# Spreading a head pair's projections one by one over the attention stage, and two output buffers for three in the expert projection (8 cores)

## What is computed

```python
xn = layernorm(x)
Q, K, V = xn @ Wq, xn @ Wk, xn @ Wv            # 16 heads of 64
alpha = softmax(Q @ K.T / 8)                   # over all keys
alpha = where(causal, alpha, 0)                # masked after the softmax
s = alpha @ V
# expert attention: 8 experts, width 128, router mask m and weights rw
q, k, v = [einsum('tc,ecd,te->td', xn, w, m) for w in (q_proj, k_proj, v_proj)]
ao = causal_softmax(q @ k.T / sqrt(128)) @ v
g = silu(einsum('td,edc,te->tc', ao, o_proj, m * rw))
out = x + s * g
```

## Time and profile before

| | |
|---|---|
| median of 2 runs | 3564.84 us (3513.45 and 3616.22) |
| the profiled execution | 3513.46 us, span 3511.6 us on its slowest core (core 6) |
| spans of the 8 cores | 3494.2 to 3511.6 us |
| TensorE matmuls | 2532.0 us busy, 72% |
| TensorE weight loads | 1156.4 us, 33% |
| VectorE | 2273.3 us, 65% |
| ScalarE | 2114.9 us, 60% |
| GpSimd | 256.7 us, 7% |

### The profile page before, as it was taken

How to read it: one execution, slowest core, us unless ns; L and a number is a source line. 1 busy time by engine, 2 the same in 40 slices (tenths; PEclk the granted TensorE clock), 3 DMA queues, 4 the chain that set the end, 5 groups by cost and what they waited for, 6 DMA issues and landing times.

```text
span 3511.6 us, 59735 instructions; the slowest of 8 cores (3494.2 to 3511.6 us)
## 1 busy us (share of the span) xinstructions
PE 2532.0 (72%) x18500; PEld 1156.4 (33%) x18642; DVE 2273.3 (65%) x5890; ACT 2114.9 (60%) x2466; POOL 256.7 (7%) x706
## 2 busy tenths in 40 slices
PE   2179997675677777777777777777777877886651
PEld 1134444332233333333333333333333333332220
DVE  7447774233366776776677677667766766776764
ACT  0000003521177986897798689779868977996762
POOL 0100000000000000010000001000000100011012
PEclk9999998898878778867877876887787578655555
DMA  5510000113200000000000000000000000003346
GB/s 154 142 40 1 1 1 1 55 52 112 83 3 3 6 6 3 4 9 3 3 6 6 3 4 9 3 3 6 6 3 4 9 3 3 6 6 113 109 147 208
DMA packets 35776, 117.11 MB, mean 33 GB/s; under 512 B 5778, under 2 KB 5778, under 8 KB 35474
## 3 DMA queue, kind: packets, MB, share of 16 engines
q1 hardware_dynamic: 22738, 71.34, 6.0%
q0 software_dynamic: 12736, 41.95, 4.1%
HBM read 79.72 MB, written 33.55 MB: 32 GB/s over the span
## 4 chain that ended last, share of the span: by engine, by line
PE 31%; ACT 21%; issue 14%; DVE 11%; another core or an unknown queue 10%; DMA 7%; DVEq 4%; POOL 0%; ACTq 0%; SPq 0%; POOLq 0%
ACT expC L1342 7%; ACT stagef L1357 6%; PE PB L887 5%; PE PB L901 5%; PE PB L872 5%; PE PB L804 4%; PE PB L759 3%; PE PB L801 3%; PE PB L816 3%; ACT stagef L1342 3%; ACT R L1357 3%; DVE tmpc L1205 2%; DMA KTt<-s_sp 2%; DVEq L1273 2%
## 5 line engine op out<-in xcount | busy, mean ns | idle before, releaser
L1205 DVE TENSOR_REDUCE tmpc<-stagef 128x2 f32<-128x1024 bf16 (+2 forms) x726 | 811.4, 1127 | 235.9 <-ACT stagef L1357 179.4
L1342 ACT ACTIVATE expC<-PB 128x1024 bf16<-128x1024 f32 x768 | 853.3, 1111 | 87.3 <-PE PB L887 87.3
L1357 ACT ACTIVATE stagef<-PB 128x1024 bf16<-128x1024 f32 x600 | 667.8, 1113 | 204.8 <-PE PB L901 132.2
L1205 DVE TENSOR_REDUCE tmpc<-R 128x2 f32<-128x1024 bf16 (+2 forms) x362 | 406.2, 1122 | 118.2 <-ACT R L1357 89.9
L1342 ACT ACTIVATE stagef<-PB 128x1024 bf16<-128x1024 f32 x384 | 429.2, 1118 | 73.4 <-PE PB L887 73.4
L887 PE MATMUL PB<-R 64*128 64x512 bf16 x1152 | 299.9, 508 | 228.2 <-ACT stagef L1357 134.5
L887 PE MATMUL PB<-QTt,KTt 64*128 64x512 bf16 x1152 | 285.8, 484 | 146.0 <-ACT stagef L1357 78.6
L1357 ACT ACTIVATE R<-PB 128x1024 bf16<-128x1024 f32 x296 | 329.9, 1114 | 81.8 <-PE PB L901 60.6
L681 PE MATMUL PB<-R,xnT 128*128 128x512 bf16 x1504 | 336.5, 380 | 2.8 <-DVE lnat L998 1.1
L1322 ACT ACTIVATE expC<-PB 128x512 bf16<-128x512 f32 x144 | 74.6, 610 | 364.3 <-remote 343.7
L901 PE MATMUL PB<-R 64*128 64x512 bf16 (+3 forms) x1088 | 265.0, 479 | 36.4 <-ACT expC L1342 19.2
(11 more groups left out here) (162 smaller groups left out, 2948.2 us busy)
## 6 DMA issues: line engine op xcount, KB each, us to landing
stagef<-x SPq DMA_DIRECT2D x64, 512.0 KB, 4.3
out<-Vau SPq DMA_DIRECT2D x32, 512.0 KB, 3.0
g_sp<-stagef SPq DMA_DIRECT2D x32, 256.0 KB, 2.0
s_sp<-s_stage POOLq DMA_DIRECT2D x64, 128.0 KB, 2.4
QTt<-g_sp POOLq DMA_DIRECT2D x32, 256.0 KB, 5.5
KTt<-s_sp POOLq DMA_DIRECT2D x32, 256.0 KB, 5.6
R<-qp POOLq DMA_DIRECT2D x8, 512.0 KB, 5.5
R<-kp POOLq DMA_DIRECT2D x8, 512.0 KB, 4.6
```

The source lines that it names most:

```text
L1205: e.tensor_reduce(s.tmpc[:].rearrange("p (h c) -> p h c", h=2)[:, :, c:c + 1], s.c1scr((m1 - 1) % 3)[:, 0:2 * kw] .rearrange("p (h k) -> p ...
L1342: e.activation(s.expCs(es), PB[[0, 1, 3][it["slot"]]][:, :], AF.Exp).then_inc(sem["aC2"], 1)
L1357: e.activation(scr[:, 0:1024], pbsrc[:, 0:1024], AF.Exp).then_inc(sem["aC1"], 1)
```

## The change

It has two parts. In `build_p3_items` a QKV item now follows every 15th C1 or C2 item, never two in one place, and not within two C2 items behind the one that ends a query block (`cool`). A place that this rule forbids is skipped. Whatever is left goes ahead of the last item of the pair. In the expert output projection the buffers are `PB[0]` and `PB[1]` in turn, not three, and the wait for the Silu is one tile tighter. Nothing else changes: the same items, the same instructions in each.

```diff
--- before.py
+++ after.py
@@ -181,14 +181,22 @@
             qk = qkv_items(p + 1)
             merged = []
             qi = 0
+            cool = 0
             for idx2, it in enumerate(base):
+                if idx2 == len(base) - 1:
+                    while qi < len(qk):
+                        merged.append(qk[qi])
+                        qi += 1
                 merged.append(it)
-                if qi < len(qk) and idx2 >= 30 and (idx2 - 30) % 14 == 0:
+                if it["kind"] == "C2":
+                    if it["t"] == 4 * it["j"] + 3:
+                        cool = 2
+                    elif cool > 0:
+                        cool -= 1
+                if (qi < len(qk) and idx2 >= 30 and (idx2 - 30) % 15 == 0
+                        and cool == 0):
                     merged.append(qk[qi])
                     qi += 1
-                    if qi < len(qk) and (idx2 - 30) % 28 == 0:
-                        merged.append(qk[qi])
-                        qi += 1
             while qi < len(qk):
                 merged.append(qk[qi])
                 qi += 1
@@ -750,9 +758,9 @@
                                    s.idt_bf[:])
             last.then_inc(sem["tT4"], 1)
             e.wait_ge(sem["aE4"], qt + 1)
-            if qt >= 3:
-                e.wait_ge(sem["aS4"], qt - 2)
-            pbo = PB[qt % 3]
+            if qt >= 2:
+                e.wait_ge(sem["aS4"], qt - 1)
+            pbo = PB[0] if qt % 2 == 0 else PB[1]
             last = None
             for ei in range(8):
                 for half in range(2):
```

## The result

The changed kernel takes 3535.08 us in the median of 43 runs (3530.65 to 3656.24), the kernel before 3516.08 us in 42 (3506.43 to 3628.03). The ratio is 1.0061, 95% interval 1.0054 to 1.0068: 21 us more. Some executions of every kernel take a few per cent longer at a lower granted clock on one die (the trace of transposes_later is of such a one): the medians hold them, and the ratios compare the others. The prediction was 3507 us, 7 us less than before: the size is small as forecast, the sign is wrong.

What follows compares the result with a forecast made beforehand. ScalarE was taken as the bound, idle while TensorE runs projection items. Per pair 52.1 us against 53.1, a gain of 1.0 over 7 pairs: 7 us off 3513.5 gives 3507 us; range 3440 to 3590 us.

Steps and rivals of the forecast that it cites:

- What bounds the kernel: Head pairs: ScalarE is the pacemaker; a pair costs its 248.6 us plus the idle time TensorE puts into it.
- Step 1, the a's: Q and K projection items, all standing alone: seven a's (all but a0) at 2.50 us, 17.5 us per pair.
- Step 1, the b's: V projection items, all standing alone: six of eight b's at 3.49 us, 20.9 us per pair.
- a0: First projection item of a pair: keeps its place and costs 5.0 us of ScalarE idle time.
- b3: V item two items behind a 6-chunk row's last chunk: VectorE adds partial sums first; 4.0 us taken, between 3.25 and 4.7.
- b7: V item before the pair's last C2 item: its cast waits for VectorE's sums; last exponential 4.8 us later, 4.7 idle.
- The old order's sum: Pair 3 before the change: ScalarE's idle time in 11 rows behind projection items sums to 53.07 us.
- The buffers: Expert output projection, two buffers for three: cost 0; if the cover went, at most 1 us for each of 32 tiles.
- Waits elsewhere: Rest of a pair's idle time, 5.7 us: drain between pairs and waits for the normalisation; the change leaves it.
- The rival that splitting loses the warm second half: Single items may each start at TensorE's lower clock: 15.3 us more per pair, 107 in all, 3620 us; chance 0.14.
- The range: Whole kernel: 3440 to 3590 us, leaving out the far half of each clock rival; own case alone 3480 to 3545.
- The rule that keeps items away from the normalisation: Order of items in the pairs: moves nothing that costs today, as old groups stand before the query block's closing C2 item.

Runs made afterwards that it cites:

- transposes_later: Changed kernel with the transposes of V taken out of the b items into an item of their own, 3 items later; 3496.8 us, ratio to before 0.9924.
- p1_two_buffers: Kernel before with only two output buffers for three in the expert projection; 3523.1 us, ratio to before 0.9985.

## Why the prediction was wrong

- *What bounds the kernel*: right. ScalarE sets the pace, its busy time per pair is the same within 0.4 us, and the result is idle time behind TensorE.
- *Step 1, the a's* (seven at 2.50 because "every a follows a lone b", from a3 and a6): this is the step that failed. What precedes an a does not make it start high: behind a lone b (a1 to a7 of the new order) 247 of 392 start low. The mean of a1 to a7 is 3.25 us, from 2.58 (a5) to 3.99 (a3): 0.75 us more for each of seven, 5.2 us per pair. Two rows of one pair were taken for a rule. Over all cores of the old trace a3b3 costs 5.40 to 6.69 us, and a3 starts low in 47 of 56 cases, though not in the pair that was read. With the means of all cores (6.20 and 5.45, less the same 3.06) the two give 2.77, which is 54.0 us per pair for 53.1 and has the right sign. The singles' own mean (3.03 from the three rows) would have given 55.8 for the measured 55.6; that is so near by luck, since its a's are 1.5 us too low per pair and its b's 1.4 too high.
- *Step 1, the b's* (3.49): 3.26 for b0, b1, b2, b4, b5 and b6, 1.4 us less per pair. Right in kind; though more of their matmuls were slow, VectorE's cast hid part of it.
- *a0* 5.0: 4.70. *b3* 4.0: 3.89. *b7* 4.7: 4.73, by the mechanism given (what the prediction calls the next scores, 1.65 us behind the cast, is the exponential that follows them; the sum doesn't change by it).
- *The old order's sum* 53.1, from one pair of one core: 52.7 over all.
- *The buffers* 0: shown by p1_two_buffers.
- *Waits elsewhere*, left as they are: right, 5.5 us per pair for 5.6.
- *The rival that splitting loses the warm second half* named the cause and the sign. Its size was wrong (107 us if every item starts low): 38% of the matmuls are slow, and not every item starts low (of the five that lost their place behind another, 218 of 280).
- *The range* of 3440 to 3590 us held.
- *The rule that keeps items away from the normalisation* moves nothing that costs, as said. From the code it has another use: the cast of an item within two C2 items behind a normalisation would stand behind it in VectorE's queue, and the normalisation waits for a product that TensorE issues only after that item. This was not tried.

## What to carry to other kernels

Where one engine waits for bursts of another, the idle time is the burst's length less what lies ready (here 8 matmuls 0.21 us apart cost 0.73 to 0.95 us, 16 some 2.5), and the burst's length depends on the clock it starts with: price single bursts by the mean over all cores and repeats, not by the two that fit. Before moving bursts about, look whether the stream between them keeps TensorE's clock up; here half as many score matmuls again, all useless, took the kernel from 0.6% slower to 1.4% faster. Two bursts in one place share one start at the lower level. When a burst is cut finer, follow the buffer of each part to the engine that frees it, and place the parts where that engine's queue is short.

## What was not expected of the hardware

- Useless matmuls shortened the kernel: ratio to before 0.986 for 1.006, with the share of slow projection matmuls down from 38% to 7% and the granted clock up from 0.77 to about 0.95.
- Between projections TensorE's clock goes up and down with nothing but scores and their products to do. In a stretch of the kernel before with no projection item (pair 3; all engines by stretch: length, TensorE matmuls, weight loads, VectorE, ScalarE, GpSimd, then the granted clock) TensorE has matmuls in flight for 67.94 of 88 us, and the granted clock is 0.66 in the mean; it changes ten times between its two levels:

```profile
2092.00:2180.00 88.00, 67.94 (x558) 28.92 (x557) 68.98 (x175) 86.65 (x97) 12.21 (x39) 0.66 0.02 6
```

While nothing but scores runs this costs next to nothing, since ScalarE keeps its pace (busy 86.65 of the 88 us); it shows only when a projection item comes.
